# Graph attention on one core: masks of two chunks turned in one go, and the end rebuilt

## The reference

```python
h = jnp.maximum(_layernorm(x, axis=-1), 0.0)        # x: (8, 2048, 256) f32
Wh = jnp.einsum('bnf,fo->bno', h, W)                # W: (256, 256)
f1 = Wh @ a[:fout, 0]
f2 = Wh @ a[fout:, 0]
e = f1[:, :, None] + f2[:, None, :]                 # (8, 2048, 2048)
e = jnp.where(e >= 0, e, ALPHA * e)
attention = jnp.where(adj > 0, e, MASK_FILL)        # adj: (8, 2048, 2048) int32
attention = jax.nn.softmax(attention, axis=1)       # over i, the rows
h_prime = jnp.einsum('bij,bjo->bio', attention, Wh)
out = x + jax.nn.elu(h_prime)
```

## Time and profile before

| what | value |
|---|---|
| median of 3 runs | 989.29 us |
| the profiled execution, its own time | 987.88 us |
| its span | 986.1 us |
| busy over the span | PE 950.0 us (96%), DVE 920.7 (93%), ACT 879.3 (89%), POOL 645.3 (65%) |
| normalise (L910), mean | 994 ns |
| root (L904), mean | 1634 ns |
| high split: L890, L893, L896, mean | 233, 586, 1902 ns |
| load of adj, issue to landing | 11.2 us (median), 64 of 1024 KB |
| row of f1, issue to landing | 6.5 us (median), 31 of 256 KB |
| the 16 transfer engines in the middle | 85% to 91% busy |

### The profile page before, as it was taken

One profiled execution on the slowest core, in us unless ns is written; L12 is line 12 of the kernel. 1 busy time (PEld: TensorE's weight loads), 2 busy tenths in 40 slices (PEclk: granted clock), 3 DMA queues, 4 the chain that ended last, 5 costly groups with the idle time before them and its releaser, 6 DMA issues.

```text
span 986.1 us, 23861 instructions
## 1 busy us (share of the span) xinstructions
PE 950.0 (96%) x8993; PEld 840.0 (85%) x8993; DVE 920.7 (93%) x1271; ACT 879.3 (89%) x1237; POOL 645.3 (65%) x676
## 2 busy tenths in 40 slices
PE   8878999999999999999999999999999999999996
PEld 6666888889888898888888888888988989898896
DVE  8799989999899998999989998999999999999975
ACT  4788989999999999999999899999999999898985
POOL 6567665776766776876767776677676775555540
PEclk8899999999999999999999999999999999999898
DMA  9477667889879889799979988979987978979724
GB/s 233 83 107 108 97 108 122 147 162 156 149 136 176 146 155 167 119 180 149 161 147 144 173 148 151 154 141 172 156 163 123 172 133 138 170 113 158 143 65 140
DMA packets 199093, 142.13 MB, mean 144 GB/s; under 512 B 7361, under 2 KB 187841, under 8 KB 198978
## 3 DMA queue, kind: packets, MB, share of 16 engines
q0 software_dynamic: 140160, 81.80, 61.5%
q1 hardware_dynamic: 58818, 58.81, 20.8%
HBM read 176.16 MB, written 16.84 MB: 196 GB/s over the span
## 4 chain that ended last, share of the span: by engine, by line
POOL 32%; PE 30%; issue 25%; DVE 5%; DMA 4%; ACT 2%; POOLq 0%; SPq 0%; DVEq 0%; ACTq 0%
POOL direct L896 10%; POOL xn L910 6%; POOL raw L882 5%; POOL inv L893 4%; PE acc L511 4%; PE acc L504 4%; PE acc L506 4%; PE tp L439 3%; PE acc_st L486 3%; PE acc_st L487 3%; PE acc_st L488 3%; POOL y L916 3%; PE pre L417 3%; POOL rstd L904 2%; POOL small_total L890 2%
## 5 line engine op out<-in xcount | busy, mean ns | idle before, releaser
L773 DVE CUSTOM_DVE_ANT_0 prob<-tp,f_row 128x2048 f32<-128x2048 bf16 x128 | 292.0, 2282 | 21.5 <-DMA f_row<-f_scratch 14.9
L590 ACT ACTIVATE prob<-prob,f 128x2049 f32<-128x2049 f32 x128 | 257.6, 2013 | 5.4 <-DVE prob L773 5.4
L486 PE MATMUL acc_st<-v,stored 128*128 128x256 f16 x960 | 261.5, 272 | 0.8 <-ACT part L620 0.8
L488 PE MATMUL acc_st<-v,stored 128*128 128x256 f16 x960 | 261.7, 273 | 0.0
L487 PE MATMUL acc_st<-v,stored 128*128 128x256 f16 x960 | 261.6, 273 | 0.0
L598 ACT ACTIVATE prob<-prob,shift 128x2048 f32<-128x2048 f32 x128 | 256.5, 2004 | 4.0
L896 POOL TENSOR_TENSOR direct<-prob,inv 128x1024 f16<-128x1024 f32 x128 | 243.5, 1902 | 10.0
L504 PE MATMUL acc<-v,direct 128*128 128x256 f16 x1024 | 233.4, 275 | 5.4 <-ACT z_direct L626 3.5
L506 PE MATMUL acc<-v,direct 128*128 128x256 f16 x1024 | 233.3, 274 | 0.0
L890 POOL TENSOR_SCALAR small_total<-total 128x1 f32<-128x1 f32 x128 | 29.8, 233 | 272.8 <-ACT prob L598 271.4
L604 ACT ACTIVATE stored<-prob,inv 128x1024 f16<-128x1024 f32 x128 | 146.1, 1142 | 47.6 <-POOL inv L893 47.6
(11 more groups left out here) (94 smaller groups left out, 1383.9 us busy)
## 6 DMA issues: line engine op xcount, KB each, us to landing
raw<-in_adj POOLq DMA_DIRECT2D x64, 1024.0 KB, 11.2
y<-in_x SPq DMA_DIRECT2D x63, 256.0 KB, 3.1
out<-y SPq DMA_DIRECT2D x63, 256.0 KB, 2.2
y<-elu POOLq DMA_DIRECT2D x56, 256.0 KB, 5.0
x_in<-in_x SPq DMA_DIRECT2D x108, 128.0 KB, 3.3
f_row<-f_scratch SPq DMA_DIRECT2D x31, 256.0 KB, 6.5
stored<-in_x SPq DMA_DIRECT2D x4, 512.0 KB, 6.9
f_scratch<-f_t SPq DMA_DIRECT2D x124, 0.5 KB
```

Source lines behind the costliest of these rows:

```text
L486: nc.tensor.matmul(bank[:, 0:FO], p_st[:, 0, rows], v_c[:, 0, :], start=(c == 0), stop=False)
L488: last = nc.tensor.matmul(bank[:, 0:FO], p_st[:, 1, rows], v_c[:, 0, :], start=False, stop=(c == G - 1))
L590: nc.scalar.activation(p_top, p_top, ACT.Prelu, bias=f2, alpha=ALPHA).then_inc(leaky, 1)
L773: nc.vector.tensor_tensor_reduce(out=prob[:, c % 2, 0:N], in0=tp_b, in1=f1_row[:, b % 2, :], scale=1.0, scalar=-3.0e38, op0=ALU.add, op1=A ...
```

## The change

The masks become bytes: 192 where there is no edge, else 0. A load holds every second row of adj for the 256 columns of two chunks, and two neighbouring columns of a row form one 16-bit element, so that one set of 16 transposes turns two chunks: the even columns are one chunk, the odd ones the other. `mask_scores` reads every second byte of `tp`, and f1 is scaled by 2^-48 beforehand and multiplied back in the same instruction. Since a chunk is now every second row of 256, x is read and y written with two neighbouring rows on a partition. Loads of adj are issued in each step for half as many rows (four buffers instead of two). Epsilon is added on GpSimd just ahead of the root, and x is normalised as (x - mean) times root, with no offset (from chunk 20 on). At the end the last six stored blocks lie in three banks, two in each, and the contributions of chunks 120 to 125 are computed before the last chunk's direct blocks; VectorE takes half of `acc` and the bank `pre`; the items are finished in one order, and x is added by GpSimd but for the last two.

```diff
-NOT_AN_EDGE = 2.0 ** 56
+F1_SCALE = 2.0 ** -48
+NOT_AN_EDGE = 192.0
...
-        raw = sb("raw", [P, 2, C, 2 * P], BF16)
+        raw = sb("raw", [P, 4, G, 2 * P], BF16)
         neg = sb("neg", [P, 2, C, P], BF16)
+        neg_bytes = neg[:].rearrange("p b m j -> p b (m j)").bitcast(U8).rearrange("p b (t q j) -> p b t q j", t=2, q=G)
...
+        tp_bytes = tp[:].rearrange("p h c -> p (h c)").bitcast(U8).rearrange("p (i t) -> p t i", t=2)
...
-            g, late = divmod(s + 19, 4)
-            return g + 1 if late == 0 and EARLY // 4 <= g < CH // 4 else None
+            return None
...
-            n = s - 9 if s <= LAST + 1 else s - 9 + EXTRA
+            n = s - 9 if s <= LAST_BATCH + G else s - 9 + EXTRA
...
+            return n < LAST_BATCH or n < LAST_BATCH + G and n % G >= EXTRA
...
+        def last_bank(pair):
+
+            return (acc_st[:], tp[:, 0, :], tp[:, 1, :])[pair - 1]
...
+        LAST_ITEMS = [4, 5, 6, 7, 0, 1, 2, 3, 8]
...
+        def x_rows(c):
+            b, j = divmod(c, C)
+            q, t = divmod(j, 2)
+            return x[b, 2 * P * q:2 * P * (q + 1), :].rearrange("(p t) f -> t p f", t=2)[t]
+
+
+        def masks_at(s):
+
+            if s < 0:
+                return [s + 5] if s >= -5 and s < -3 else []
+            return [2, 3] if s == 0 else ([s + 3] if s + 3 < CH else [])
...
-            def transpose_mask(c):
-                pe.wait_ge(neg_ready, c + 1)
-                if c == 0:
+            def transpose_masks(pair):
+                pe.wait_ge(neg_ready, 2 * pair + 2)
+                if pair == 0:
                     pe.wait_ge(ident_ready, 1)
-                wait(pe, scores, c)
+                wait(pe, scores, 2 * pair)
                 for m in range(C):
-                    last = nc.tensor.transpose(tp_b[:, m * P:(m + 1) * P], neg[:, c % 2, m, :], ident_b[:])
+                    last = nc.tensor.transpose(tp_b[:, m * P:(m + 1) * P], neg[:, pair % 2, m % 2 * G + m // 2, :],
+                                               ident_b[:])
                 last.then_inc(tp_ready, 1)
...
+            def last_blocks(pair, chunks):
+                pe.wait_ge(lo_stored, chunks.stop)
+                if chunks.start == SECOND:
+                    if pair == 1:
+                        pe.wait_ge(part_ready, firsts(SECOND - 1))
+                    else:
+                        pe.wait_ge(scores, CH)
+                for c in chunks:
+                    p_st = stored[:, c // G % 2, c % G]
+                    v_c = v[:, c % RV]
+                    for h in range(2):
+                        rows = slice((2 * pair + h) * P, (2 * pair + h + 1) * P)
+                        z = last_bank(pair)[:, h * FO:(h + 1) * FO]
+                        nc.tensor.matmul(z, p_st[:, 0, rows], v_c[:, 0, :], start=(c == SECOND and h == 0), stop=False,
+                                         skip_group_check=True)
+                        nc.tensor.matmul(z, p_st[:, 0, rows], v_c[:, 1, :], start=False, stop=False,
+                                         skip_group_check=True)
+                        last = nc.tensor.matmul(z, p_st[:, 1, rows], v_c[:, 0, :], start=False, stop=(c == LAST),
+                                                skip_group_check=True)
+                if chunks.stop == CH:
+                    last.then_inc(last_done, 1)
...
+                if s == LAST:
+                    last_blocks(1, range(SECOND, LAST - 1))
+                if chunk(s + 1) and s % 2 == 1:
+                    transpose_masks((s + 1) // 2)
                 if chunk(s + LEAD + 1):
                     transpose_x(s + LEAD + 1)
                 if chunk(s - 1):
                     direct_blocks(s - 1)
+            last_blocks(2, range(SECOND, LAST - 1))
+            last_blocks(3, range(SECOND, LAST - 1))
+            direct_blocks(LAST)
+            extra_blocks(LAST - 1)
+            extra_blocks(LAST)
+            for pair in range(1, 4):
+                last_blocks(pair, range(LAST - 1, CH))
...
+            act.wait_ge(tp_ready, TURNED)
+            take_direct(B - 1, 0)
+            for k in last_items:
+                finish_relu(k)
+                finish_exp(k)
...
-            def make_mask(c):
-                pair = c // 2
-                dve.wait_ge(raw_in[pair % 2], 16 * (pair // 2 + 1))
-                wait(dve, tp_ready, c - 1)
-                nc.vector.tensor_scalar(neg[:, c % 2], raw[:, pair % 2, :, c % 2 * P:(c % 2 + 1) * P], 0.0, -NOT_AN_EDGE, ALU.is_le, ALU.mult
-                                        ).then_inc(neg_ready, 1)
+            def make_masks(n):
+                pair, t = divmod(n, 2)
+                dve.wait_ge(raw_in[n % 4], 16 * (n // 4 + 1))
+                wait(dve, tp_ready, pair - 1)
+                nc.vector.tensor_scalar(neg_bytes[:, pair % 2, t], raw[:, n % 4], 0.0, NOT_AN_EDGE,
+                                        ALU.is_le, ALU.mult).then_inc(neg_ready, 1)
 
             def mask_scores(c):
                 b, j = divmod(c, C)
-                dve.wait_ge(tp_ready, c + 1)
+                dve.wait_ge(tp_ready, c // 2 + 1)
                 if j == 0:
                     dve.wait_ge(f1_row_in[b % 2], 64 * (b // 2 + 1) - (16 if b % 2 == 0 else 0))
                 if c == 0:
                     dve.wait_ge(f1_last, 1)
                 wait(dve, lo_stored, c - 1)
                 nc.vector.tensor_tensor_reduce(
-                    out=prob[:, c % 2, 0:N], in0=tp_b, in1=f1_row[:, b % 2, :], scale=1.0, scalar=-3.0e38,
-                    op0=ALU.add, op1=ALU.max, accum_out=prob[:, c % 2, N:N + 1]).then_inc(scores, 1)
+                    out=prob[:, c % 2, 0:N], in0=tp_bytes[:, c % 2, :], in1=f1_row[:, b % 2, :], scale=-1.0 / F1_SCALE,
+                    scalar=-3.0e38, op0=ALU.subtract, op1=ALU.max, accum_out=prob[:, c % 2, N:N + 1]).then_inc(scores, 1)
...
+                if c == LAST:
+                    low_stored()
...
+            def take_direct_late():
+                dve.wait_ge(direct_done, CH)
+                dve.wait_ge(elu_ready, summed_by_dma)
+                nc.vector.tensor_scalar(z_direct[:, 4:8, :].rearrange("p m o -> p (m o)"),
+                                        acc[:, 4:8, :].rearrange("p m o -> p (m o)"), k_out, None, ALU.mult
+                                        ).then_inc(z_direct_late, 1)
+
+            def take_extra():
+                dve.wait_ge(extra_done, C)
+                nc.vector.tensor_scalar(part[:, 0:EXTRA, :].rearrange("p m o -> p (m o)"), pre[:], k_out, None, ALU.mult
+                                        ).then_inc(z_extra, 1)
+
+            def add_last(pair):
+                dve.wait_ge(last_done, pair)
+                dve.wait_ge(part_ready, firsts(SECOND - 1))
+                z = part[:, 2 * pair:2 * pair + 2, :].rearrange("p m o -> p (m o)")
+                nc.vector.scalar_tensor_tensor(out=z, in0=last_bank(pair), scalar=k_out, in1=z, op0=ALU.mult, op1=ALU.add
+                                               ).then_inc(z_last, 1)
...
+            take_direct_late()
+            take_extra()
+            late = 1
+            for k in last_items:
+                finish_elu(k)
+                if late < 4:
+                    add_last(late)
+                    late += 1
...
-            def load_raw(pair):
-                wait(pool, neg_ready, 2 * pair - 2)
+            def load_raw(n):
+                pair, t = divmod(n, 2)
+                wait(pool, neg_ready, n - 3)
                 b, q = divmod(pair, C // 2)
-                nc.gpsimd.dma_start(raw[:, pair % 2], adj[b].rearrange("(c p) j -> p c j", p=P)[
-                    :, :, 2 * P * q:2 * P * (q + 1)]).then_inc(raw_in[pair % 2], 16)
+                nc.gpsimd.dma_start(raw[:, n % 4], adj[b].rearrange("(q p t) j -> t p q j", p=P, t=2)[
+                    t, :, :, 2 * P * q:2 * P * (q + 1)]).then_inc(raw_in[n % 4], 16)
...
-                pool.wait_ge(var_s, i + 1)
                 wait(pool, xn_ready, chunks.stop - RS)
                 rs = slice(chunks.start % RS, chunks.start % RS + len(chunks))
+                if chunks.start >= EARLY:
+                    pool.wait_ge(mv_s, chunks.stop)
+                    nc.gpsimd.tensor_scalar(var_eps[:, rs], mv[:, rs, 1], EPS, None, ALU.add).then_inc(var_s, 1)
+                pool.wait_ge(var_s, i + 1)
...
+                else:
+                    pool.wait_ge(rstd_s, root_index(c) + 1)
+                    nc.gpsimd.tensor_scalar(xn_buf(c), x_buf(c), mv[:, c % RS, 0:1],
+                                            rstd[:, c % RS:c % RS + 1], ALU.subtract, ALU.mult).then_inc(xn_ready, 1)
...
+            def add_x(k):
+                pool.wait_ge(elu_ready, k + 1)
+                pool.wait_ge(x_last_in[k - summed_by_dma], 16)
+                pair = y_buf(k).rearrange("p t f -> p (t f)")
+                nc.gpsimd.tensor_tensor(pair, pair, e_buf(k), ALU.add).then_inc(y_ready, 1)
...
+                if s >= -1 and chunk(s + 5):
```

(1 more changed line is left out.)

207 lines of the change are left out of this document (102 added, 105 removed).

## The result

| | before | after |
|---|---|---|
| median of 4 runs, us | 990.96 (988.13 to 994.96) | 1016.93 (1016.62 to 1018.67) |
| ratio, 95% interval | | 1.0254 [1.0222, 1.0286] |
| profiled execution, its span | 987.88, 986.1 | 1016.72, 1014.9 |

The change makes the kernel 2.5% slower. The forecast was 980, range 963 to 1006: the sign is wrong and the time lies outside.

What follows compares the result with a forecast made beforehand. Three engines had nearly the same step: TensorE 7.23, VectorE 7.25, ScalarE 7.19 us. 987.88 + 0 (middle) - 5.6 (last batch) - 3.8 (end) = 978.5, the median 1.4 higher: 980; own range 971 to 984, with rivals 963 to 1006.

Steps and rivals of the forecast that it cites:

- so I take 0.05 instead of 0.30: Middle, VectorE: stops of the mask by GpSimd fall from 0.30 to 0.05 us a step, giving 7.30 against 7.31.
- Rival 1: Middle: VectorE and GpSimd hold each other, the mask keeps the full 0.30 of stops; step 7.55, time 1003; chance 0.22.
- Normalise costs the same: GpSimd: normalise keeps its form of two scalars, costs the same (1.0 us) and no longer waits for an offset.
- at most 0.3, under 0.1 a step: GpSimd: the epsilon instruction, one every fourth step, takes at most 0.3 us, under 0.1 a step.
- at most 5.9, not a bound: GpSimd's work a step: 5.16 us plus 0.3 to 0.65 for load issues, at most 5.9, so not a bound.
- cover is nearly gone in every fourth step ... I charge nothing: GpSimd before small_total: 4.2 us of work in a 4.4 gap, overrunning by 0.7 with y's issue; charged nothing.
- Alone this gives little: Middle, TensorE: halved transposes save 0.45 us a step, leaving 6.79, but ScalarE at 7.19 is next.
- The mask's size: VectorE: the mask with byte output takes 1.14 us from start to start, 0.53 more than now.
- rivals 2 and 3: VectorE's mask: bytes cost nothing, 970, chance 0.12; or bytes go at one element a cycle, about 1100, chance 0.05.
- 6.6 after, still under 7.03: nothing: First batch: VectorE's work rises from 6.1 to 6.6 us a step, under the 7.03 between scores, so no change.
- ScalarE ... 6.5, and sets the pace: Last batch: ScalarE needs 6.5 us a step against 6.87 measured and sets the pace; 15 steps give -5.6.
- ScalarE's chain is the bound, and additions on GpSimd go beside it: The end: ScalarE's chain bounds, GpSimd's additions run in parallel; the span ends at 982.3 instead of 986.1, -3.8 us.

Runs made afterwards that it cites:

- a_oldnorm: The changed kernel with epsilon and offset back on VectorE and x again normalised as x times root plus offset: 1006.86 us, ratio 1.0150.
- c_form: The changed kernel with its normalisation's operations turned to multiply-add on the same operands, so the values differ: 1006.05 us, ratio 1.0124.
- n_multsub: The changed kernel with GpSimd making mean times root for four chunks and normalising as x times root minus that product: 1024.75 us, ratio 1.0323.
- r_split: The kernel before with each load of adj issued as two halves: 990.01 us, ratio 0.9984.
- b_newnorm: The kernel before with only epsilon on GpSimd and x normalised as (x - mean) times root, from chunk 20 on: 993.99 us, ratio 1.0018.
- p_half: The kernel before with only one of the mask's 16 transposes made in every second step: 978.02 us, ratio 0.9846.
- m_bytes: The kernel before with only its mask written as bytes, all 16 transposes a step kept: 1014.97 us, ratio 1.0224.
- f_bytes: The changed kernel with the load of adj casting to bytes and the mask one multiply-add on 1024 16-bit pairs: 982.32 us, ratio 0.9894.
- g_both: The changed kernel with byte-casting load and 16-bit pair mask, old normalisation with epsilon and offset on VectorE, and x added by VectorE at the end: 970.36 us, ratio 0.9777.
- k_order: The changed kernel with VectorE making the mask after the low splits instead of before them: 1040.04 us, ratio 1.0476.

## Why the prediction was wrong

By stretch, from the starts of the scores of the two profiled executions:

| stretch | forecast | measured |
|---|---|---|
| up to the first scores | 0 | 33.63 - 32.1 = +1.5 |
| first batch | 0 | 16 x (7.174 - 7.03) = +2.3 |
| middle | 0 | 96 x (7.555 - 7.306) = +23.9 |
| last batch | -5.6 | 15 x (6.938 - 6.869) = +1.0 |
| the end | -3.8 | 37.2 - 37.1 = +0.1 |
| sum | -9.4 | +28.8 |

**The step that failed most** is "so I take 0.05 instead of 0.30" for the stops of the mask. The mask's work was sized well (+0.53; least time 1194 against 675, +0.52). But from start to start it took 1.463, not 1.14 + 0.05: 0.27 too little a step, 26 us, which is the middle's loss (23.9 against the kernel before). The other terms of VectorE's sum came as forecast: 6.00 for the rest and 0.09 of waits. The argument for 0.05 was that GpSimd and ScalarE would run ahead; GpSimd did the reverse. The stops did not shrink from 0.30, they came to 0.32, and moved: in the table of steps by four, mask and "direct" now meet in the step behind the root, where before they did not. Rival 1 kept the full stops and gave 7.55 for the middle, which is what came. In part that is luck: it assumed the old cost of the normalisation, and with that (a_oldnorm) the stops are 0.17 and the step 7.41. Its 1003 left the gains of the last batch and the end standing, and these failed too.

**Why GpSimd was not ahead** are three terms and one that I put at nothing. "Normalise costs the same" failed: the form with a subtraction takes 1.23 and not 0.55, shown by c_form and n_multsub; with stops it is 1.07 more a step. Epsilon on GpSimd was "at most 0.3, under 0.1 a step" and takes 762 ns in mean, 0.19 a step. The issues of the loads were sized within their bounds (1114 ns, +0.50 a step), and r_split shows that they cost nothing on the kernel before, where GpSimd has slack. Together GpSimd works 7.555 - 0.57 = 6.98 a step where I wrote "at most 5.9, not a bound". The term at nothing is "cover is nearly gone in every fourth step ... I charge nothing": that step went from 6.74 to 7.43, with ScalarE's wait for the inverse up from 0.64 to 1.67. With the old normalisation it is 6.96 and 0.92, so most of this too hangs on the form. Replacing the normalisation alone gives back 10 of the 26 us (a_oldnorm). The lever is the pair of engines: on the kernel before, the new normalisation moved 0.150 off VectorE and gave it 0.228 back as stops (b_newnorm); on the changed one it is 0.042 and 0.152 (a_oldnorm).

**The transposes.** "Alone this gives little" held: 0.09 to 0.16 a step (p_half), and up to 0.15 under a byte mask (a_oldnorm beside m_bytes). **The mask's size** held, and with it rivals 2 and 3 fell (393 ns is reached only with 16-bit elements). The Trainium skill (VectorE: DVE Perf Modes, The perf-mode tier table) has 1227 ns for 2048 elements at the rate of two a cycle, which the prediction took from there; the traces agree, with 1194 at least in the changed kernel and a median of 1227 in m_bytes. **The scores** kept 2278 ns.

**The first batch.** "6.6 after, still under 7.03: nothing" failed: it is 7.17 (7.13 in m_bytes), with a short mask 6.90 and 6.74 (f_bytes, g_both). So the sum of VectorE's work alone did not tell its pace there. The step behind the root is again longer, 7.97 against 7.19, and three such steps are 2.3 us; what else changed there cancels out. But the long mask is not the only cause, for p_half, with the old mask, has 7.17 as well. Its rows show a low granted clock, the number behind the five engines:

```profile
50.00:75.00 25.00, 20.12 (x149) 15.88 (x149) 24.05 (x32) 21.19 (x28) 15.94 (x16) 0.86 0.73 106
75.00:100.00 25.00, 18.90 (x114) 14.12 (x114) 24.39 (x32) 19.52 (x28) 18.62 (x19) 0.80 0.69 101
```

From 30 to 50 us the mean granted clock is 0.83 in both kernels. In the kernel before, with TensorE 75% busy there, it is 1.00 in the two stretches that follow; in p_half, with TensorE 67% busy there, it is 0.86 and 0.80, which means part of them at the lower of its two levels. The changed kernel has 0.86 and 1.00. What this costs was not tried by itself. The 1.5 us before the first scores is not explained either: kernels with the old mask have 0.5 to 1.0 of it too (b_newnorm, p_half, r_split).

**The last batch.** "ScalarE ... 6.5, and sets the pace" failed. With TensorE relieved and the old mask it was 6.83 (p_half), with the new mask 6.94, with the short one 6.72 and 6.68. So the longer mask ate TensorE's relief, which was 0.04 a step between the two profiles, and even the short one stays over 6.5; what holds it there is open.

**The end.** The matmuls went as worked out: ScalarE takes `acc` 996.33 - 977.74 = 18.6 after the last scores, where I had 968.1 - 949.0 = 19.1. "ScalarE's chain is the bound, and additions on GpSimd go beside it" failed. VectorE's chain is the bound, with 1.98 us for an item with a late bank (two passes and a late bank, all 0.6 to 0.7), and GpSimd's additions do not go beside it but in turn with it, 1.9 an item. ScalarE needs 1.2. So the end took 37.2 from the start of the last scores where I had 33.3.

## What to carry to other kernels

Time taken off the busiest engine is worth what the next ones have to spare: some 0.4 off TensorE gave 0.09 to 0.16 a step. When two engines stop each other, price an edit by what it does to both: a longer instruction on one side also holds the other, and an edit that moves work from one to the other can lose it all again. Where work comes only in every fourth step, sum that step by itself: a mean over all steps hides that there is no slack left in it. Before moving work to an engine "with slack", read the duration of exactly the pair of operations and types that the new instruction uses, or time it by itself.

## What the runs showed of the hardware

- GpSimd's instruction on 128 x 256 f32 with two scalars per partition: multiply-add 548 ns at least, subtract-multiply 1232, multiply-subtract 1234.
- VectorE's mask of 2048 elements, at least: bf16 to bf16 675 ns, bf16 to bytes 1194; the same 2048 bytes as 1024 elements of 16 bits, 393.
- Issuing a load of half as many rows costs GpSimd 994 ns in mean instead of 1305 (r_split against before): halving it saves a quarter. Beside the byte mask both are longer: 1503 for the whole (m_bytes), 1114 to 1232 for the half (after, a_oldnorm).
- Small instructions are held as long ones are: four numbers on GpSimd took 2.04 us beside VectorE's low split and mask (k_order), and one number 0.81 at 663.34 in the changed kernel.
